# Loading the gate stage's weights during the last attention unit, and dividing that unit on VectorE

## The reference

```python
q, k, v = (src @ w).reshape(b, s, h, hd).transpose(0, 2, 1, 3)   # 16 heads of 16, for q_w, k_w, v_w
scores = einsum('bhqd,bhkd->bhqk', q, k) / sqrt(hd) * scale[..., None]
out = einsum('bhqk,bhkd->bhqd', softmax(scores), v)              # back to (b, s, 256)
gate = sigmoid(out @ gate_w + gate_b)
attn = out * gate @ out_w
x = _ln(src + attn, n1_g, n1_b)
logits = xr @ moe_gate_w + moe_gate_b                            # top 2 of 8, the larger index is used
sel = expert(chosen)(xr)                                         # 256 -> 512, norm, gelu, -> 256
result = _ln(x + sel * weights, n2_g, n2_b)
```

## Time and profile before

| | |
|---|---|
| median of 3 runs | 2515.07 us |
| the profiled execution, its own time | 2515.51 us |
| its span in the trace | 2513.7 us |
| TensorE busy | 2399.9 us, 95% |
| VectorE busy | 2099.4 us, 84% |
| ScalarE busy | 1799.9 us, 72% |
| GpSimd busy | 996.8 us, 40% |
| attention's last matmul issued to the gate stage's first | 2140.05 to 2146.68 us |
| the gate stage | 2146.6 to 2281.7 us |

### The profile page before, as it was taken

How to read it: one execution, slowest core, us unless ns; L and a number is a source line. 1 busy time by engine, 2 the same in 40 slices (tenths; PEclk the granted TensorE clock), 3 DMA queues, 4 the chain that set the end, 5 groups by cost and what they waited for, 6 DMA issues and landing times. The chain is left out here.

```text
span 2513.7 us, 45435 instructions
## 1 busy us (share of the span) xinstructions
PE 2399.9 (95%) x16377; PEld 1043.6 (42%) x16377; DVE 2099.4 (84%) x4149; ACT 1799.9 (72%) x2369; POOL 996.8 (40%) x1191
## 2 busy tenths in 40 slices
PE   7899999999789999999999999999999999897996
PEld 5566665555443223222222222232222232574554
DVE  7778888989688998998999898999999993373887
ACT  4887887777225878877787787787888788542664
POOL 1777878988731222221221212112210111354654
PEclk9999999999889999999999999999999999888998
DMA  3322333323230311203040040040030000225883
GB/s 113 121 75 87 99 95 94 102 88 105 85 94 14 56 22 32 46 14 52 14 63 2 14 64 8 7 64 14 22 43 2 1 2 1 92 69 219 281 289 104
DMA packets 105908, 174.09 MB, mean 69 GB/s; under 512 B 21194, under 2 KB 80610, under 8 KB 100548
## 3 DMA queue, kind: packets, MB, share of 16 engines
q1 hardware_dynamic: 97924, 155.20, 23.3%
q0 software_dynamic: 6016, 14.49, 1.5%
q10 hardware_dynamic: 1744, 1.50, 0.2%
HBM read 145.21 MB, written 27.02 MB: 69 GB/s over the span
## 5 line engine op out<-in xcount | busy, mean ns | idle before, releaser
L1674 DVE TENSOR_REDUCE max_part<-round_psum 128x1 f32<-128x512 f32 x2048 | 1269.4, 684 | 105.0 <-PE round_psum L1583 99.9
L1639 ACT ACTIVATE p_exp<-score_psum 128x1024 f32<-128x1024 f32 x1024 | 993.4, 1022 | 215.5 <-PE score_psum L1568 210.0
L1583 PE MATMUL round_psum<-k_stack,q_stack 64*128 64x512 bf16 x2048 | 706.5, 384 | 11.0 <-DVE max_part L1674 6.6
L1559 PE MATMUL score_psum<-q_stack,k_stack 64*128 64x512 bf16 x2048 | 599.5, 379 | 0.9 <-ACT p_exp L1639 0.2
L1568 PE MATMUL score_psum<-q_stack,k_stack 35*128 35x512 bf16 x2048 | 595.0, 378 | 0.0
L1614 PE MATMUL pv_psum<-p_exp,values 128*17 128x512 f32 x4096 | 540.4, 599 | 0.0
L1583 PEld LDWEIGHTS round_psum<-k_stack,q_stack 64*128 64x128 bf16 x2048 | 189.6, 93 | 602.4 <-DVE max_part L1674 511.9
L671 PE MATMUL rot<-tokens_t,w_in 128*128 128x512 f32 x576 | 272.6, 605 | 0.2
L1568 PEld LDWEIGHTS score_psum<-q_stack,k_stack 35*128 35x128 bf16 x2048 | 189.0, 94 | 116.4 <-issue 1.1
L1709 POOL TENSOR_TENSOR rden<-pv_out,minus_one 128x16 f32<-128x16 f32 x32 | 92.9, 2902 | 358.3 <-ACT pv_out L1657 356.0
L1695 POOL CAST max_parts<-max_neg 128x16 bf16<-128x16 f32 x96 | 20.4, 213 | 367.5 <-DVE max_neg L1680 345.1
(11 more groups left out here) (284 smaller groups left out, 3500.8 us busy)
## 6 DMA issues: line engine op xcount, KB each, us to landing
expert_w<-in_expert_w SPq DMA_DIRECT2D x39, 1028.0 KB, 5.2
cum_rows_in<-cum_rows SPq DMA_DIRECT2D x64, 512.0 KB, 3.8
cum_pairs_in<-cum_rows SPq DMA_DIRECT2D x240, 64.0 KB, 2.8
qk_rows<-qk_parts SPq DMA_DIRECT2D x64, 192.0 KB, 3.2
q_stack<-qk_rows SPq DMA_DIRECT2D x84, 128.0 KB, 8.3
k_stack<-qk_rows SPq DMA_DIRECT2D x84, 128.0 KB, 9.4
token_rows<-tokens SPq DMA_DIRECT2D x12, 512.0 KB, 3.6
tokens<-in_x SPq DMA_DIRECT2D x8, 512.0 KB, 9.2
```

Of the source, the lines that this page charges most:

```text
L1559: nc.tensor.matmul(ebank[i // 2][:, i % 2, :], ks[rows, n % 2, plane, k * P:(k + 1) * P], qs[rows, n % 2, plane, q * BLK:(q + 1) * BLK], s ...
L1583: nc.tensor.matmul(bank[step][:, :], qs[rows, n % 2, plane, at:at + P], ks[rows, n % 2, plane, keys * BLK:(keys + 1) * BLK], start=True, s ...
L1639: nc.scalar.activation(pt[:, (k * 2 + pair) % 4, :, :], ebank[pair][:, :, :], ACT.Exp).then_inc(*exped.up(u, k, pair))
L1674: nc.vector.tensor_reduce(mx[:, c * HG + h, keys:keys + 1], bank[step][:, :], AX_X, ALU.max).then_inc(*maxed.up(u, k, i))
```

## The change

Three things are done. First, a class `GateInputs` places the eight inputs and the first block of source rows into slot 0 of `k_stack`, and SP issues these nine DMAs in the attention stage, behind its last DMA of row maxima; ACT no longer issues any at the start of the gate stage, and SP's string begins with `load1 load2`. Second, the last unit's `turn_out` goes to DVE, which reads the transposed sum straight from PSUM: one reciprocal and four products; ACT's second copy and POOL's five operations fall away for that unit. Third, `BUSY5` has 2 matmuls on zeros ahead of the first gate product where it had 10. The key stack now stays allocated until the program's end.

```diff
@@ attention
+            sp_.wait_ge(*scored.at(NU - SB - 1, KT - 1, 1))
+            for name in GATE_LOADS:
+                nc.sync.dma_start(G.weights[name], io[name]).then_inc(*G.loaded.up(name))
+            sp_.wait_ge(*x1_saved.all())
+            nc.sync.dma_start(G.x1[:, :, :], x1_dram[:, 0:CPB, :]).then_inc(*G.x1_load[0].up(0))
...
-                if what == "turn_out":
+                if what == "turn_out" and u < NU - 1:
                     act.wait_ge(*out_turned.at(u))
                     nc.scalar.copy(pvs[:, :], bank[step][:, :]).then_inc(*out_in.up(u))
...
+                if what == "turn_out" and u == NU - 1:
+                    n, q = UNITS[u]
+                    b, g = GROUPS[n]
+                    o = bank[step][:, :].rearrange("p (n w) -> p n w", w=32)
+                    ve.wait_ge(*out_turned.at(u))
+                    ve.wait_ge(*divided.at(u - 1))
+                    nc.vector.reciprocal(rden[:, :].unsqueeze(2), o[:, :, HD:HD + 1]).then_inc(*last_inverse.up(u))
+                    ve.wait_ge(*last_inverse.at(u))
+                    for c in range(CPB):
+                        nc.vector.tensor_tensor(heads(attn[:, b * KT + q * CPB + c, g * HG * HD:(g + 1) * HG * HD],
+                                                          HG, HD), o[:, c * HG:(c + 1) * HG, 0:HD],
+                                                    over_last(rden[:, c * HG:(c + 1) * HG], HD), ALU.mult)
...
-                if what == "turn_out":
+                if what == "turn_out" and u < NU - 1:
                     n, q = UNITS[u]
                     b, g = GROUPS[n]
                     o = pvs[:, :].rearrange("p (n w) -> p n w", w=32)
@@ gate stage
-    "SP": "load2 load0 load1 load3 rows0 load4 rows1 load5 rows2 load7 rows3 load6 rows4 rows5 rows6 rows7",
+    "SP": "load1 load2 load3 rows0 load4 rows1 load5 rows2 load7 rows3 load6 rows4 rows5 rows6 rows7",
-BUSY5 = {"gate0": 10, "place1": 2, ...
+BUSY5 = {"gate0": 2, "place1": 2, ...
+class GateInputs:
+    def __init__(self, sems, place):
+        shapes = {"gate_w": (KD, D), "attn_out_w": (KD, D), "router_w": (KD, NE), "gate_b": (KD,), "n1": (2, D),
+                  "router_b": (NE,), "iotas": (I_AT["scale"].stop,), "expert_b": (FF + D,)}
+        self.weights, at = {}, 0
+        for name in GATE_LOADS:
+            shape = shapes[name]
+            t = place[0:NE if name == "expert_b" else P, at:at + math.prod(shape)]
+            at += math.prod(shape)
+            self.weights[name] = heads(t, *shape) if len(shape) == 2 else t
+        self.x1 = heads(place[:, at:at + CPB * D], CPB, D)
...
-    x1 = sb("x1_block", [P, 3, CPB, D])
+    x1 = [G.x1, *(sb(f"x1_block{i}", [P, CPB, D])[:, :, :] for i in range(1, 3))]
...
-            sp_.wait_ge(*x1_saved.all())
...
-            for name, t in zip(GATE_LOADS, (w_gate[:, :, :], w_o[:, :, :], w_r[:, :, :], gb[:, :], rowsv[:, :, :],
-                                            b_r[:, :], iotas[:, :], rest[:, :])):
-                nc.scalar.dma_start(t, io[name]).then_inc(*gate_load.up(name))
@@ build
+            ks = sb(late, "k_stack", [P, 2, HG, SEQ], BF16)
+            G = GateInputs(sems, ks[:, 0, :, :].rearrange("p h s -> p (h s)").bitcast(F32))
```

More of the change, by code:

```diff
@@ L1 @@
 import itertools
+import math
 from contextlib import ExitStack
@@ L1037, in __init__ @@
         self.qs = sb("q_stack", [P, 2, HG, SEQ], BF16)
-        self.ks = sb("k_stack", [P, 2, HG, SEQ], BF16)
+        self.ks = ks
         self.w_qk = sb("w_qk", [P, KD, NG, 3 * HG * HD])
@@ L1448, in attention_order, with attention @@
         yield from due.get(t, [])
-def attention(nc, sems, ctx, K, io, attn, srcT, S, V, src_mv, src_rstd, x1_dram, x1_saved):
+def attention(nc, sems, ctx, K, io, attn, srcT, S, V, src_mv, src_rstd, x1_dram, x1_saved, G):
     def sb(name, shape, dt=F32):
@@ L1503, in attention @@
     out_turned = sems.events("out_turned", range(NU))
-    denominator = sems.events("denominator_inverse", range(NU))
-    divided = sems.events("out_divided", range(NU))
+    denominator = sems.events("denominator_inverse", range(NU - 1))
+    divided = sems.events("out_divided", range(NU - 1))
+    last_inverse = sems.events("last_denominator_inverse", [NU - 1])
     out_in = sems.events("out_stored", range(NU))
@@ L1753 @@
 }
-BUSY5 = {"gate0": 10, "place1": 2, "place3": 14, "logits5": 2, "rows6": 4, "place5": 2, "logits6": 1}
+BUSY5 = {"gate0": 2, "place1": 2, "place3": 14, "logits5": 2, "rows6": 4, "place5": 2, "logits6": 1}
+class GateInputs:
[9 more added lines that the diff above has]
+        self.x1 = heads(place[:, at:at + CPB * D], CPB, D)
+        self.loaded = sems.dma("gate_load", GATE_LOADS)
+        self.x1_load = [sems.dma(f"x1_load{i}", range(i, NBLK, 3)) for i in range(3)]
 class Routes:
@@ L1780, in ps @@
         return ctx.enter_context(nc.psum_tensor(name, shape, dt))
[L1782 to L1788, removed]
+    w_gate, w_o, w_r, gb, rowsv, b_r, iotas, rest = (G.weights[name] for name in GATE_LOADS)
+    x1_load, gate_load = G.x1_load, G.loaded
+    x1 = [G.x1, *(sb(f"x1_block{i}", [P, CPB, D])[:, :, :] for i in range(1, 3))]
     iota = {n: iotas[:, at] for n, at in I_AT.items()}
@@ L1902, in _ @@
                         g = b * CPB + i
-                        e = nc.scalar.activation(x1[:, b % 3, i, :], x1[:, b % 3, i, :], ACT.Identity,
+                        e = nc.scalar.activation(x1[b % 3][:, i, :], x1[b % 3][:, i, :], ACT.Identity,
                                                  bias=shift[:, g:g + 1], scale=src_rstd[:, g:g + 1])
@@ L2034, in _ @@
                         ve.wait_ge(*attn_in.at(b, half))
-                        nc.vector.tensor_tensor(res[:, three, i, :], x1[:, three, i, :],
+                        nc.vector.tensor_tensor(res[:, three, i, :], x1[three][:, i, :],
                                                 heads(abank[half][:, :], 2, D), ALU.add).then_inc(*summed.up(b, half))
@@ L2520, in build @@
         sems.clear()
-        with ExitStack() as att:
-            V = sb(att, "values", [P, NCH, AH, VW])
-            S = Stacks(nc, sems, att, turned)
-            attention(nc, sems, att, K, io, main, turned, S, V, src_mv, src_rstd, tokens_by_p[:, :, D:], x1_saved)
-        sems.clear()
-        R = Routes(nc, sems, ctx)
-        with ExitStack() as stage:
-            gate_and_route(nc, sems, stage, K, io, main, turned, tokens_by_p, x1_saved, src_mv, src_rstd, R, rec_dram,
-                           xr_saved, scattered)
-        with ExitStack() as stage:
-            experts(nc, sems, stage, K, io, R, tokens_dram, rec_dram, xr_saved, scattered, out)
+        with ExitStack() as late:
+            ks = sb(late, "k_stack", [P, 2, HG, SEQ], BF16)
+            G = GateInputs(sems, ks[:, 0, :, :].rearrange("p h s -> p (h s)").bitcast(F32))
+            with ExitStack() as att:
+                V = sb(att, "values", [P, NCH, AH, VW])
+                S = Stacks(nc, sems, att, turned, ks)
+                attention(nc, sems, att, K, io, main, turned, S, V, src_mv, src_rstd, tokens_by_p[:, :, D:], x1_saved, G)
+            sems.clear()
+            R = Routes(nc, sems, late)
+            with ExitStack() as stage:
+                gate_and_route(nc, sems, stage, K, io, main, turned, tokens_by_p, x1_saved, src_mv, src_rstd, R, rec_dram,
+                               xr_saved, scattered, G)
+            with ExitStack() as stage:
+                experts(nc, sems, stage, K, io, R, tokens_dram, rec_dram, xr_saved, scattered, out)
 def layout(a):
```

9 lines of the change are left out of this document (3 added, 6 removed).

## The result

The changed kernel took 2501.20 us (median of 4 runs, 2497.80 to 2506.86), against 2514.88 for the kernel before beside it (4 runs, 2514.43 to 2518.87). The ratio is 0.9948, interval 0.9932 to 0.9963. The forecast was 2506.7 with a range of 2503.3 to 2510.0. The direction was right; 8.4 us were forecast, 13.7 came, and the time lies outside the range. In two later comparisons the same changed kernel was 0.9963 (0.9951 to 0.9975) and 0.9958 (0.9944 to 0.9972) of the kernel before. Weighted by their intervals the three make 0.9958, some 10.6 us of 2514 (8.6 to 12.6). So there are two questions: what is wrong in the sum of 8.4, and how much of the 13.7 is this change at all.

The account below looks back on a forecast made before the run. The seam was taken as a one-at-a-time chain and the gate stage as bound by TensorE. 3.74 + 2.95 + 2.82 - 1.1 = 8.4 off the profiled 2515.51 gave 2507.1, as median 2506.7; range 2503.3 to 2510.0.

Parts of the forecast that it names:

- Division: End of attention: VectorE's reciprocal and four products replace ScalarE's copy and GpSimd's operations, ending 3.74 us earlier (bounds 0.7 to 4.0).
- ScalarE's eight DMAs: Start of the gate stage: without these issues ahead of ScalarE's copies, TensorE's 2.95 us idle ahead of block 1 goes.
- Eight zeros and the clock: Ahead of the first gate product: dropping eight zeros gains 2.82 us; gate products at low clock lose 1.1.
- The first rival: TensorE's restart at the gate stage: clock stays low longer, losing 2.55 us, not 1.1; 2508.2 to 2509, chance 0.20.
- SP's loads, the dead keys: Nine loads issued by SP in attention into `k_stack`: nothing becomes late, no gain counted.
- the slower rival: VectorE in the gate stage: operands in the dead keys run at half speed; 2524 us (2519 to 2530), chance 0.03.
- the loads in front of the maxima: End of attention: SP's loads go ahead of the last row maxima, losing 2.8 us; 2509.5, chance 0.04.
- Passed on behind: From the first gate product to the experts' first zeros: the earlier start, 8.4 us, is passed on whole.
- the bounds of the clock's loss: First gate products at low clock: none lost if it rises with the first product, 2.55 us if it rises late.
- a rival with 0.08: Meeting ahead of the gate stage: the clock does not fall, so transposes and zeros run faster; 2503.4 us, chance 0.08.

Follow-up runs that it names:

- 2: Kernel before with only `k_stack` allocated first and kept to the end, no instruction moved; 2514.94 us, ratio 1.0015 to the kernel before.
- 3: Kernel before with 9 instead of 6 buffers for the experts' output rows (`V_RING`); 2512.25 us, ratio 1.0006 to the kernel before.
- run 5: Kernel before with only the last attention unit's division moved to VectorE, straight from PSUM; 2507.10 us against 2512.61, ratio 0.9983.
- run 6: Changed kernel with GpSimd's division put back and ten zeros, so only the loads are moved; 2505.92 us, ratio 0.9979 to the kernel before.
- 7: Changed kernel with ten zeros instead of two ahead of the first gate product; 2503.02 us, ratio 0.9962 to the kernel before.
- run 1: Changed kernel measured again, nothing edited; 2502.33 us against 2509.68 for the kernel before, ratio 0.9963.
- 9: Changed kernel measured a third time, nothing edited; 2502.27 us against 2513.42 for the kernel before, ratio 0.9958.
- run 4: Changed kernel with 9 instead of 6 buffers for the experts' output rows (`V_RING`); 2499.72 us, ratio 0.9956 to the kernel before.
- run 10: Changed kernel without the last two zeros ahead of the first gate product; 2501.46 us against 2513.42 for the kernel before, ratio 0.9950.
- run 8: Changed kernel with four zeros behind attention's last transposes and six before the semaphores are cleared; 2499.11 us against 2512.61 for the kernel before, ratio 0.9952.
- run 11: Changed kernel with three and four zeros across the meeting, none ahead of the first gate product; 2502.10 us against 2513.42 for the kernel before, ratio 0.9957.

## Why the prediction was wrong in size

The seam of every kind, and when the clock was low there:

| kernel | A to F | F to G | A to G | clock low at the seam |
|---|---|---|---|---|
| before | 7.29 | 10.33 | 17.62 | 13.65 |
| 2, only the keys' place | 7.27 | 11.97 | 19.24 | 13.65 |
| 3, before with more buffers | 7.27 | 11.78 | 19.05 | 13.65 |
| 5, division alone | 3.47 | 10.60 | 14.07 | 10.24 |
| 6, loads alone | 7.14 | 5.77 | 12.91 | 6.82 |
| 7, both, ten zeros | 3.33 | 5.66 | 8.99 | 3.41 |
| changed kernel (first, 1, 9) and run 4 | 3.33 | 3.90 to 3.92 | 7.23 to 7.25 | 3.41 |
| 10, no zeros | 3.33 | 3.07 | 6.40 | 3.41 |
| 8, zeros across the meeting | 3.65 | 2.72 | 6.37 | none |
| 11, fewer of them | 3.33 | 2.29 | 5.62 | none |

The parts add up: the division alone gains 3.55 and the loads alone 4.71, together 8.26; both in one kernel with ten zeros gain 8.63; the zeros add 1.76, which is 10.39. Step by step against the prediction:

- **Division: right, 3.74 forecast, 3.96 measured** (A to F, 7.29 to 3.33). The reciprocal took 0.26 where I took 0.20, the products 0.62 for 0.70, and the meeting 1.73 for 1.86. The Trainium skill (VectorE: DVE Perf Modes, section "First, the fixed hardware budget") gave a repeat count of 8 for the reciprocal, and with it some 0.12 more than 0.20. 0.26 lies between the two figures, nearer to mine; neither mattered.
- **ScalarE's eight DMAs: the 2.95 of idle time was right for that profile and too small as a price.** In two of the four executions that have these issues and were profiled (before, 2, 3 and 5) the idle time is 5.4 to 5.6. The prediction took the shorter one from its only profile. The longer ones make A to G 1.4 to 1.6 longer; how often they come in the runs that were not profiled isn't on record.
- **Eight zeros and the clock: this step of the sum failed.** I booked 2.82 for the zeros at their mixed speed and gave back 1.1, since the rise was to come 1.6 to 3.1 behind the first dense work, at up to 2149.7. Together 1.7. Measured: from the zeros' start to the product 3.68 before and 0.43 after, 3.25, and no product at the low level. The premise that failed is that only the zeros and products count as dense work and transposes do not bring the clock up. It rose at 2145.64, before the zeros began at 2145.72, with sixteen transposes in a row as the only work since the restart.

  In run 6 it rose at 2145.10, 0.16 behind the start of the zeros and with 3.5 us of transposes ahead of them. In runs 1, 4 and 9 it fell only when TensorE was back at work (0.5 to 0.7 behind the restart) and rose 3.41 later, at the first gate product; there the transposes take less and the two zeros run low, and F to G is the same. That transposes alone suffice rests on the first profile.

  The idle time ahead of block 1 goes with a clock that stays low until 2156.39 before: without it and with the meeting as it was (run 6) the low stretch is 6.82 and not 13.65. So moving the loads has two gains, the idle time itself and 1.6 us of zeros and transposes that ran faster, and I booked one. The first rival, the clock low for longer, fell with it. The Trainium skill (TensorE: Matmul & The Clock Gate, section "Part 4: PE-mode transpose") backed it: transposes in that mode do not count as busy the way matmuls do. Here the first profile of the changed kernel disagrees, where the rise at 2145.64 came over transposes alone; the profile lists them as MATMUL and does not show whether that mode was on.
- **SP's loads, the dead keys: right, at nothing.** 1222 and 686 ns as before (1222 and 684), and TensorE's wait for the last maxima is 0.2 in both kernels; the slower rival and the loads in front of the maxima are out.
- **Passed on behind: roughly.** From G to Z it is 124.75 before and 124.42 after; VectorE's first sum came at 2159.33, 10.86 earlier where 8.4 were forecast, and was still ended by `a_psum`.

With 3.96, 2.95, 3.25 and 0.23 from the transposes the seam gains 10.39; the three comparisons make 10.6 (8.6 to 12.6) of the whole.

**The rest of the 13.7.** In the profiled pair the spans differ by 8.6: 0.47 ahead of A, 10.39 from A to G, 0.33 from G to Z, and 2.59 lost from Z to the end. Averaged over the executions with either seam and no other edit ahead of the experts (before, 2, 3 against after, 1, 9), A to G gains 11.4, G to Z 0.8, and Z to the end loses 1.8 (232.0 to 233.8): 10.4 in all. Both later stretches vary between profiles that have the same instructions there, G to Z from 119.9 to 125.2 and Z to the end from 230.6 to 235.0. For G to Z the trace shows where. But for run 10, whose first products were slower, all kernels run alike to 0.1 us for 46 us behind G. The clock is low for the first time behind G after 48 to 50 us in runs 2, 3, 6, 7, 8, 10 and 11, for 3.4 us (6.8 in run 8), and after 71 to 72 us in the others; 3.4 us low cost 1.7. From 85 to 90 us on each has long low stretches that lie differently. From G to Z the mean granted clock was 0.87 in run 5, 0.84 in the kernel before and 0.83 in run 8, and the stretch took 119.94, 124.75 and 125.24. The windows of the kernel before and of run 5, each for 4 us from the last zeros into `rank_psum`:

```profile
2252.31:2256.31 4.00, 4.00 (x18) 0.50 0.02 5
```
```profile
2247.03:2251.03 4.00, 4.00 (x28) 0.78 0.06 11
```

The kernel before gets 18 matmuls done in 4 us, run 5 28, and from G to Z run 5 needs 119.94 for what took 124.75. Such a stretch comes and goes without any edit near it; whether the earlier start has a part in it isn't shown.

Behind Z two things show. TensorE waits 12 to 13 us behind Z for the first rows of the experts: 0.5 to 1.7 us in the kernel before, in runs 2, 5, 6, 7 and 8 and in the changed kernel's first profile, 1.9 to 2.6 us in runs 1, 3, 4, 9, 10 and 11. In these six and no others the clock then falls once more, for 3.41 us. In run 1:

```profile
2279.82 0.44 PE L2349 MATMUL e_t<-const_f,expert_rows_in 128*128 128x128 f32 x2 [2.02 <-DMA expert_rows_in<-token_rows,expert_records]
```
```profile
2280.87:2284.28 3.41, 3.41 (x7) 0.50 1.02 417
```

Z to the end is 233.0 to 235.0 in the six and 230.6 to 232.0 in the others, but for the changed kernel's first profile with 234.5. In that one the chain of waits between 2300 and 2470 goes five times through a store of `token_out` of 8.1 to 8.7 us, and TensorE is idle five times for ScalarE there, 0.16 to 0.75 each, 1.86 together; the other profiles have two such stores in that part of the chain at most, and runs 2 to 5 and 7 none. By that chain the stores do cost time in a single execution, though more buffers move no median by what can be measured. What decides how often either comes stays open.

My range was too narrow. The seam's 10.39 alone, off 2515.07, makes 2504.7, which lies inside it; the other 3.5 us must come of how the four runs of each kernel fell in the later stretches and, by up to 1.6, of the longer issues, and which of these it was in the runs without a profile isn't known. The range held the bounds of the clock's loss, and of its gain only a rival with 0.08; and the 0.2% that a comparison can tell is 5 us, more than what I had left on the fast side (3.4).

## What to carry to other kernels

An idle gap on TensorE behind a restart can be paid twice, once as itself (2.95 us here) and once as the work behind it that still runs at the low level (1.6 here); when a gap goes, work out anew when the clock rises, and don't carry the old moment over. Matmuls on zeros that cover a load were worth only their full-speed time, 0.22 each, once the load was early and the clock up. For a change of a few us measure the seam's own stretch in several profiles, since the total moves by as much for reasons that have nothing to do with it.

## What the runs showed of the hardware that was not expected

- The low stretch at the seam was 3.41 us long in six profiles, in which it began with TensorE's restart or up to 0.7 behind it, 6.82 in run 6, 10.24 in run 5, and 13.65 in the kernel before and runs 2 and 3.
- The clock rose over transposes alone, 3.4 us behind the restart (one profile), and did not fall over a meeting in which TensorE ran ten zeros (run 8) or seven (run 11).
- A DMA's issue on ScalarE, else 0.40 to 0.69 us, took 1.8 to 2.0 for two of eight in two of four profiles with the same eight issues.
- A reciprocal of 128x16 from PSUM took 0.26 us on VectorE and four products of 128x64 0.62, where GpSimd took 2.90 for the power and 1.05 for the products.
